# Layer 1 as one stream of 32 attention items, with its layer norms inside

## The chip, the cores and the metric

One core of one Trainium2 chip. The metric is the device time of one execution in microseconds, the median over runs. The kernel before: 1745.28 us, median of 3 runs (1742.61 to 1745.62).

## The reference, cut to what matters

The program is four cross-attention layers in a row on a token tensor of 32 x 64 tokens by 256 (2048 tokens in all), with a context tensor of the same shape. The change is in layer 1:

```
h = layer_norm(x, ln1);  x = x + cross_attention(h, context, w1)     # 16 heads of 128
h = layer_norm(x, ln2);  x = x + cross_attention(h, context, w2)     # same shapes
h = layer_norm(x, ln_mlp); x = x + gelu(h @ w_fc1 + b_fc1) @ w_fc2 + b_fc2   # 256 -> 1024 -> 256
cross_attention: q = h@wq+bq, k = c@wk+bk, v = c@wv+bv, a 65th key and value (bias_k, bias_v) per head
                 softmax(q k / sqrt(128)) v, then @ wo + bo, over groups of 64 queries and 64 keys (+1)
```

Layers 0, 2 and 3 compute other forms of cross-attention; layer 3 ends with an MLP of the same shape as layer 1's. Their arithmetic stays as it is.

## The kernel before, in words

A phase is a set of five instruction streams (one for each engine) between two barriers over all engines. Phases follow one another: setup (`phase_setup`), layer 0 (`phase_layer0`), then for layer 1: features 1, attention 1, features 2, attention 2, features 3 and MLP 1; then the plain features, attention and MLP of layers 2 and 3, and the store.

**Features** (`phase_features`, lines 411 to 629). Four blocks of 512 tokens. DVE aggregates the statistics and normalizes (L590, L597), GpSimd makes the inverse deviation (L502, L504), TensorE transposes 8 squares per block (L524), ScalarE applies scale and offset and rounds to the high part (L559, L565), DVE subtracts to the low part (L607). The attention's features phase also loads its weights and makes 17 bias rows, with 17 float32 products on TensorE (L539, L541; the rows are called `bvo`).

**Attention** (`phase_layer1_attention`, lines 653 to 1016). An item is one block of 512 tokens and one group of 4 heads; 16 items, written out by hand as a pipeline. In iteration j TensorE runs: scores of item j-1 (L772), the first half of context of item j-2 (L828), half the values of item j-1 (L811), the second half of context, the other half of values, outputs of item j-2 (L844), queries and keys of item j (L797). Each float32 product in projections is three products of high and low parts. The context product takes, for each pair of batches and head, two matmuls of 64 rows by 64 columns each (one per batch). DVE turns the probabilities with 16 transposes of 32 partitions per item (L960). In the last group of heads (4 items) TensorE also transposes the kept bias probabilities (L781) and adds one product with `bvo` to each output (L847), and DVE takes the new statistics (L986). GpSimd splits the next group's weights (L722, L724) and SyncE loads them. Every engine takes its work in the order written.

**MLP** (`phase_mlp`, lines 1042 to 1151). TensorE first transposes the bias rows (L1077); then per block 8 products up (L1089), and 8 down (L1101) two steps later. GpSimd adds the second bias to all of `x_res` at the start, and joins the halves of the context.

**Setup** (`phase_setup`). SyncE issues 10 DMAs for the rows of constants (L158), TensorE transposes them (L194), DVE copies them to `cols` (L240), and only then normalizes the tokens for layer 0 (L249).

Of the kernel before, what the change touches and what calls it, by code (L numbers as in the profile page):

```python
# [105 lines left out]
CONST_ROWS = ("bq", "bk", "bias_k", "bias_v", "bv")  # L106


def phase_setup(nc, A, G):
# [4 lines left out]
    with Mem(nc, "su", G.psum) as m:  # L114
# [7 lines left out]
        rows = m.sb("rows", [5 * H1, 2, P])  # L122
# [3 lines left out]
        cols_ps = m.ps("cols_ps", (P, 2, 5 * H1))  # L126
# [8 lines left out]
        rows_in, cols_psum = m.sem("rows_in"), m.sem("cols_psum")  # L135
# [3 lines left out]
        with nc.Block() as block:  # L139
            @block.sync  # L140
            def _(sp):
# [35 lines left out]
            def _(pe):  # L177
# [13 lines left out]

                pe.wait_ge(rows_in, 16 * 2 * len(CONST_ROWS))
                for i in range(2):
                    mm = pe.transpose(cols_ps[:, i, :], rows[:, i, :], G.ident[0:5 * H1, 0:5 * H1])  # L194
# [17 lines left out]
            def _(dve):  # L212
# [27 lines left out]
                dve.tensor_copy(G.cols[:, :, :], cols_ps[:, :, :])  # L240
# [13 lines left out]
def phase_layer0(nc, A, G):  # L254
# [6 lines left out]
    with Mem(nc, "l0", G.psum) as m:  # L261
# [16 lines left out]
        y_psum, y_done, o_psum, x_done = (m.sem(n) for n in ("y_psum", "y_done", "o_psum", "x_done"))  # L278
        STEPS = PAIRS // 2
        with nc.Block() as block:  # L280
            @block.gpsimd
            def _(pool):
                def body(j, front, back):
# [127 lines left out]
def phase_features(nc, G, tag, src, dst_hi, dst_lo, kind, eps=0.0, scale=None, offset=None,  # L411
                   update=False, mlp=None, loads=(), have_stats=True,
                   attention=None):
# [10 lines left out]


    with Mem(nc, tag, G.psum) as m:
        affine = m.sb("affine", [P, 2, KT])
        row_in = m.sb("row_in", [2 * KT, P])
        stats = G.stats if have_stats else m.sb("stats", [P, PAIRS, 6])
        mv = m.sb("mv", [P, PAIRS, 2])  # L430
        rstd = m.sb("rstd", [P, PAIRS])
        normed = m.sb("normed", [P, PAIRS, D])
        raw = [m.sb(f"raw{i}", [P, BLK]) for i in range(2)]
        feat_ps = [m.ps(f"feat_ps{i}", (P, BLK)) for i in range(3)]
        affine_ps = m.ps("affine_ps", (P, 2 * KT))
        affine_in, stats_done, mv_done, eps_added, rstd_done, normed_done = (m.sem(n) for n in
            ("affine_in", "stats_done", "mv_done", "eps_added", "rstd_done", "normed_done"))
        feat_psum, raw_done, hi_done, lo_done = (m.sem(n) for n in ("feat_psum", "raw_done", "hi_done", "lo_done"))
        affine_psum, affine_done, rows_zero = m.sem("affine_psum"), m.sem("affine_done"), m.sem("rows_zero")
        if update:  # L440
            spread_affine = m.sb("spread_affine", [P, 2, D])
            spread_in, scaled = m.sem("spread_in"), m.sem("scaled")
        arrived = m.sem("arrived")
        if attention:
            i_att, wo_dram, bo_dram = attention
            wo, bo = m.sb("wo", [P, H1, D]), m.sb("bo", [1, D])
            lhs, unit = m.sb("lhs", [P, H1, H1 + 1]), m.sb("unit", [1, H1 + 1])
            bvo_ps = m.ps("bvo_ps", (H1 + 1, D))
            wo_in, cleared, unit_zero, lhs_done, bvo_psum = (m.sem(n) for n in
                ("wo_in", "cleared", "unit_zero", "lhs_done", "bvo_psum"))  # L450
        if mlp:
            w_in, w_high = [m.sem(f"w_in{n}") for n in range(2)], m.sem("w_high")
            small_in = m.sem("small_in")
        normalized = src if kind == "plain" else normed
        with nc.Block() as block:
            @block.sync
            def _(sp):
                if scale is not None:
                    sp.wait_ge(rows_zero, 1)
                    sp.dma_start(row_in[0:KT, :], scale.rearrange("(k p) -> k p", p=P)).then_inc(affine_in, 16)  # L460
                    if offset is not None:
                        sp.dma_start(row_in[KT:2 * KT, :], offset.rearrange("(k p) -> k p", p=P)).then_inc(affine_in, 16)
                if update:
                    for n, v in enumerate((scale, offset)):
                        sp.dma_start(spread_affine[:, n, :], v.rearrange("(o n) -> o n", o=1).partition_broadcast(P)).then_inc(spread_in, 16)
                if attention:
                    sp.dma_start(wo[:, :, :], wo_dram.rearrange("(h d) n -> d h n", d=K1)).then_inc(wo_in, 16)
                    sp.dma_start(bo[:, :], bo_dram.rearrange("(o n) -> o n", o=1)).then_inc(wo_in, 16)
# [161 lines left out]

class Operands:
    pass


# [1442 lines left out]
```

## Time and profile before

| | |
|---|---|
| Median of 3 runs | 1745.28 us |
| The profiled execution: time, span | 1738.92 us, 1737.2 us |
| TensorE, busy | 1585.5 us (91%) |
| DVE, ScalarE, GpSimd busy | 1128.0, 668.4, 433.6 us |
| Mean granted TensorE clock | 0.960 |
| First product of attention 1 to first product of MLP 1 | 143.61 to 1153.20 us |

Times within the execution are microseconds from its first instruction. A matmul in float32 is two records of TensorE. "Busy" of TensorE is the union of its records, each of which lasts longer than its share since they overlap: what one costs is read from start to start.

### The profile page before, as it was taken

The page shows a single profiled execution, that of the slowest core. Times are in us where ns is not written, and L with a number is a line of the kernel's source. Part 1 is how long each engine was busy: PE and PEld are TensorE (multiplying, and loading weights), DVE is VectorE, ACT ScalarE, POOL GpSimd, SP SyncE. Part 2 cuts the span into 40 slices and gives each one's busy share as a digit, 9 for nine tenths or more (in the row PEclk, how much of TensorE's full clock was granted, in tenths as well). Part 3 has the DMA queues.
Part 4 walks back from the last instruction along what each step waited for, and adds up shares of the span by engine and source line. Part 5 has one row for each costly group of instructions (what it writes and reads, how often), then busy time and mean ns, then how long its engine had stood idle before and what let it go on. Part 6 is the DMA issues. An engine that isn't in the chain of part 4 may idle for free. (4 is left out here: it accounts for less than half of the span.)

```text
span 1737.2 us, 35121 instructions
## 1 busy us (share of the span) xinstructions
PE 1585.5 (91%) x14252; PEld 1335.9 (77%) x14252; DVE 1128.0 (65%) x2358; ACT 668.4 (38%) x1201; POOL 433.6 (25%) x518
## 2 busy tenths in 40 slices
PE   5979999999999979999999999869878968999797
PEld 3656888888888758888888888758866747888597
DVE  6875666666666655666666666675489955676443
ACT  4654333333333234333333333242256633444321
POOL 2012020110200021110200200081068866763400
PEclk9999999999999979999999999969989978999899
DMA  3011010000000021010000100020140000000001
GB/s 102 1 54 55 2 49 2 25 26 1 25 13 1 1 80 31 19 32 1 26 26 1 38 1 1 1 71 1 17 118 2 2 1 2 2 3 2 1 0 48
DMA packets 48471, 38.35 MB, mean 22 GB/s; under 512 B 10626, under 2 KB 45384, under 8 KB 48200
## 3 DMA queue, kind: packets, MB, share of 16 engines
q1 hardware_dynamic: 48328, 36.30, 7.2%
q8 instruction: 107, 1.75, 0.4%
q14 instruction: 36, 0.29, 0.1%
HBM read 34.20 MB, written 2.10 MB: 21 GB/s over the span
## 5 line engine op out<-in xcount | busy, mean ns | idle before, releaser
L960 DVE STREAM_TRANSPOSE att_pt<-att_prob 32x256 f32<-32x256 f32 x512 | 222.8, 435 | 6.6
L914 ACT ACTIVATE att_q_sb<-psum,split_cols 128x512 f32<-128x512 f32 x128 | 88.1, 688 | 307.7 <-PE psum L797 307.7
L844 PE MATMUL psum<-att_wo_hi,att_ot_hi 128*128 128x256 f32 x512 | 150.4, 294 | 2.8 <-DVE g_x_res L983 2.8
L931 DVE TENSOR_REDUCE att_rmax<-psum 128x6 f32<-128x390 f32 (+1 forms) x96 | 49.2, 513 | 158.1 <-PE psum L772 158.1
L844 PE MATMUL psum<-att_wo_lo,att_ot_hi 128*128 128x256 f32 x512 | 145.8, 285 | 0.0
L844 PE MATMUL psum<-att_wo_hi,att_ot_lo 128*128 128x256 f32 x512 | 145.7, 285 | 0.0
L828 PEld LDWEIGHTS psum<-att_pt,att_v_sb 64*128 64x128 f32 x2048 | 122.2, 191 | 19.3 <-issue 17.7
L828 PE MATMUL psum<-att_pt,att_v_sb 64*128 64x64 f32 x2048 | 131.1, 279 | 4.9 <-DVE att_ot_lo L973 4.9
L917 ACT ACTIVATE att_k_sb<-psum,split_cols 128x512 f32<-128x512 f32 x128 | 88.1, 688 | 92.4 <-PE psum L797 92.4
L973 DVE TENSOR_TENSOR att_ot_lo<-psum,att_ot_hi 128x1024 fp32r<-128x1024 f32 x64 | 78.4, 1225 | 68.2 <-ACT att_ot_hi L880 68.2
L983 DVE TENSOR_TENSOR g_x_res<-psum,g_x_res 128x256 f32<-128x256 f32 x128 | 54.2, 423 | 101.5 <-PE psum L844 78.8
L722 POOL CAST att_wqk_hi<-w_stage_qk 128x512 fp32r<-128x512 f32 x28 | 17.1, 611 | 383.9 <-PE psum L797 382.2
L797 PE MATMUL psum<-split_feat_hi,att_wqk_hi 128*128 128x512 f32 x256 | 102.2, 399 | 6.4 <-POOL att_wqk_lo L741 6.4
L811 PE MATMUL psum<-att_wv_hi,split_ctx_hi 128*128 128x512 f32 x256 | 107.5, 420 | 0.1
L880 ACT ACTIVATE att_ot_hi<-psum 128x1024 fp32r<-128x1024 f32 x64 | 65.6, 1025 | 106.5 <-PE psum L828 106.5
L797 PE MATMUL psum<-split_ctx_hi,att_wqk_hi 128*128 128x512 f32 x256 | 102.2, 399 | 0.0
L844 PEld LDWEIGHTS psum<-att_wo_hi,att_ot_hi 128*128 128x128 f32 x512 | 97.6, 191 | 5.6 <-issue 3.5
L797 PE MATMUL psum<-split_ctx_lo,att_wqk_hi 128*128 128x512 f32 x256 | 101.9, 398 | 0.0
L797 PE MATMUL psum<-split_feat_hi,att_wqk_lo 128*128 128x512 f32 x256 | 101.3, 396 | 0.0
L797 PE MATMUL psum<-split_ctx_hi,att_wqk_lo 128*128 128x512 f32 x256 | 101.3, 396 | 0.0
L797 PE MATMUL psum<-split_feat_lo,att_wqk_hi 128*128 128x512 f32 x256 | 101.1, 395 | 0.0
L811 PE MATMUL psum<-att_wv_hi,split_ctx_lo 128*128 128x512 f32 x256 | 100.9, 394 | 0.0
(292 smaller groups left out, 4059.3 us busy)
## 6 DMA issues: line engine op xcount, KB each, us to landing
ln_wo<-in_L_xattn_wo SPq DMA_DIRECT2D x2, 2048.0 KB
w_stage_qk<-in_L_xattn_wq SPq DMA_DIRECT2D x32, 128.0 KB, 2.3
w_stage_qk<-in_L_xattn_wk SPq DMA_DIRECT2D x32, 128.0 KB, 2.4
w_stage_vo<-in_L_xattn_wv SPq DMA_DIRECT2D x8, 512.0 KB, 4.2
w_stage_vo<-in_L_xattn_wo SPq DMA_DIRECT2D x8, 512.0 KB, 3.9
c_ctx_tok<-in_ctx SPq DMA_DIRECT2D x4, 512.0 KB, 5.2
g_x_res<-in_x SPq DMA_DIRECT2D x4, 512.0 KB, 8.2
m_w<-in_L_xattn_w_fc SPq DMA_DIRECT2D x2, 1024.0 KB, 8.5
```

The source lines that it names most:

```text
L722: pool.tensor_copy(hi, raw).then_inc(w_hi, 1)
L797: mm = pe.matmul(dst[:, :], a, b, start=(k == 0 and t == 0), stop=(k == KT - 1 and t == 2))
L811: mm = pe.matmul(v_ps[p % 2][:, :], a, b, start=(k == 0 and t == 0), stop=(k == KT - 1 and t == 2))
L828: mm = pe.matmul(c_ps[:, u, p % 2, h, :], v_sb[rows, p, h * K1:(h + 1) * K1], pt[rows, h, pp, p % 2, :], start=True, stop=True)
L844: mm = pe.matmul(o_ps[p % 2], a, b, start=(h == 0 and t == 0), stop=(not last and h == HG - 1 and t == 2))
L880: act.activation(by_half(ot_hi, pp), c_ps[:, :, :, :, :].rearrange("p u c h t -> p u (c h) t"), ACT.Copy).then_inc(ot_high, 1)
L914: act.activation(q_sb[:, h, :], q_ps[:, :], ACT.Identity, bias=G.cols[:, i - 1, head:head + 1]).then_inc(q_ready, 1)
L917: act.activation(k_sb[:, h, :, 0:T], k_ps[:, :].rearrange("p (b t) -> p b t", t=T), ACT.Identity, bias=G.cols[:, i - 1, H1 + head:H1 + hea ...
L931: dve.tensor_reduce(rmax[:, a:b], s_ps[group][:, :, :], X_AXIS, ALU.max).then_inc(max_done, 1)
L960: turned = dve.transpose(pt[to:to + 32, :, :, r, 32 * a:32 * a + 32].rearrange("p h a t -> p (h a) t"), by_pair[of:of + 32, :, u, 32 * c:3 ...
L973: dve.tensor_tensor(by_half(ot_lo, pp), c_ps[:, :, :, :, :].rearrange("p u c h t -> p u (c h) t"), by_half(ot_hi, pp).bitcast(F32), ALU.su ...
L983: dve.tensor_tensor(G.x_res[:, pair, :], o_ps[p % 2], G.x_res[:, pair, :], ALU.add).then_inc(x_added, 1)
```

## The change

Layer 1 is one phase, `phase_layer1`, over 32 items (16 per attention), followed by MLP 1. The item pipeline is the one above with these edits.

- The features of a block are made inside the iterations: `norm_at(j)` gives block 0 to 3 at j = -1 to 2, 4 to 7 at j = 15 to 18, 8 to 11 at j = 31 to 34. TensorE transposes the 8 squares after the queries and keys of head 1; ScalarE does 4 operations of 128x512 there; DVE normalizes before it adds outputs; the low part is GpSimd's, in blocks 0 and 11 DVE's. The transposes write into the banks of the scores.
- Bias rows: in the second iteration of each group of heads TensorE makes 4 x 2 rows (`bias_outputs`, 8 float32 matmuls of 2 weight columns each, at partitions 32h), ScalarE copies them, 4 small DMAs place them. The bias probabilities have 33 columns for 17.
- The context product is one matmul of 128 rows by 128 columns per pair of batches and head, with zeros in the blocks off the diagonal; its high and low parts are taken in four steps of 128x512 for two of 128x1024. The outputs wait for all four.
- The last item's probabilities are turned by TensorE and ScalarE.
- The first attention weights are loaded during layer 0; MLP 1's first matrix at the end of the stream, split on ScalarE and GpSimd; its second matrix is split at the start of MLP 1.
- The scales, offsets and MLP biases come as more rows in setup: 8 more DMAs and two more small DVE operations there. The MLPs' own transposes of the bias go.
- In the MLPs GpSimd's additions are spread over the products.

```diff
-            for i in (1, 2):
-                with Mem(nc, f"w{i}") as mw:
-                    w = attention_operands(mw, A, i)
-                    phase_features(nc, G, f"ln{i}", G.x_res, *feat, "ln", 1e-5,
-                                   A[f"L1_xattn_ln{i}_scale"], A[f"L1_xattn_ln{i}_offset"], loads=w.loads,
-                                   attention=(i, A[f"L1_xattn_wo{i}"], A[f"L1_xattn_bo{i}"]))
-                    phase_layer1_attention(nc, A, G, i, w)
-            with Mem(nc, "m1") as mm:
...
-                phase_features(nc, G, "ln3", G.x_res, *feat, "ln", 1e-5,
-                               A["L1_xattn_ln_mlp_scale"], A["L1_xattn_ln_mlp_offset"], mlp=mlp)
-                phase_mlp(nc, G, "mlp1", *feat, mlp, ACT.Gelu, join_context=True, loads=layer2.loads)
+            mlp = layer1_mlp_operands(ms, G, A)
+            phase_layer1(nc, A, G, layer1, mlp)
+            phase_mlp(nc, G, "mlp1", *feat, mlp, G.cols[:, 0, 5 * H1 + 3 * KT:ROWS], ACT.Gelu, join_context=True, split_w2=True,
+                      loads=layer2.loads)
...
+        def norm_at(j):
+            n, b = divmod(j + 1, NG * NBLK)
+            return NBLK * n + b if j >= -1 and b < NBLK and n <= LAYERS else None
...
                 def context(j, pp):
...
                     for p in (2 * pp, 2 * pp + 1):
+                        if pp:
+                            pe.wait_ge(ot_ready, PPB * j + p - 1)
                         for h in range(HG):
-                            for u in range(2):
-                                rows = slice(T * u, T * u + T)
-                                mm = pe.matmul(c_ps[:, u, p % 2, h, :], v_sb[rows, p, h * K1:(h + 1) * K1],
-                                               pt[rows, h, pp, p % 2, :], start=True, stop=True)
-                    mm.then_inc(c_psum, 1)
+                            mm = pe.matmul(c_ps[:, p % 2, h, :], v_sb[:, p, h * K1:(h + 1) * K1],
+                                           pt[:, h, pp, p % 2, :, :].rearrange("p u t -> p (u t)"), start=True, stop=True)
+                        mm.then_inc(c_psum, 1)
...
+                def features(blk, j):
+                    pe.wait_ge(normed_done, PPB * (blk + 1))
+                    if j > 0:
+                        pe.wait_ge(shifted, len(GROUPS) * min(j, NI))
+                    if blk:
+                        pe.wait_ge(raw_done, KT * blk)
+                    if j >= NI:
+                        pe.wait_ge(pt_copied, 4)
+                    for k in range(KT):
+                        for i in range(PPB):
+                            mm = pe.transpose(f_ps[k][:, i * P:(i + 1) * P], normed[:, i, k * P:(k + 1) * P], G.ident[:, :])
+                        mm.then_inc(feat_psum, 1)
+
+                def bias_outputs(g, j):
+                    layer, gl = divmod(g, NG)
+                    pe.wait_ge(wo_ready, g + 1)
+                    pe.wait_ge(shifted, len(GROUPS) * j)
+                    for n, part in enumerate((wo_hi, wo_lo)):
+                        for h in range(HG):
+                            mm = pe.matmul(bvo_ps[32 * h:32 * h + 2, :], G.lhs[:, layer, HG * gl + h, :],
+                                           part[:, h, :].bitcast(F32), start=(n == 0), stop=(n == 1))
+                    mm.then_inc(bvo_psum, 1)
...
+                for j in range(-1, NI + 3):
+                    new, old, now = 1 <= j <= NI, 2 <= j <= NI + 1, norm_at(j)
+                    if new:
                         scores(j - 1)
+                    if old and last_group(j - 2):
+                        turn_bias(j - 2)
+                    if old:
                         context(j - 2, 0)
+                    if new:
                         values(j - 1, 0)
+                    if old:
                         context(j - 2, 1)
+                    if new:
                         values(j - 1, 1)
+                    if j == NI:
+                        turn(NI - 1)
+                    if old:
                         outputs(j - 2)
                     for h in range(HG):
+                        if 0 <= j < NI:
                             queries_keys(j, h)
+                        if h == 1 and now is not None:
+                            features(now, j)
+                        if h == 2 and 0 <= j < NI and j % NBLK == 1:
+                            bias_outputs(j // NBLK, j)
```

ScalarE's operations on a block of features, which stand between its copies of head 1 and of head 2; DVE's order (it stands after the values are kept); and the rows in setup:

```diff
+                def features(blk):
+                    cols = slice(blk % NBLK * BLK, (blk % NBLK + 1) * BLK)
+                    for k in range(KT):
+                        act.wait_ge(feat_psum, KT * blk + k + 1)
+                        if blk:
+                            act.wait_ge(feat_ready, KT * (blk - 1) + k + 1)
+                        scale, offset = affine(blk, k)
+                        act.activation(raw[:, k, :], f_ps[k][:, :], ACT.Identity, bias=offset, scale=scale).then_inc(raw_done, 1)
+                    for k in range(KT):
+                        act.wait_ge(raw_done, KT * blk + k + 1)
+                        act.activation(G.feat_hi[:, k, cols], raw[:, k, :], ACT.Copy).then_inc(hi_done, 1)
...
+                    if now is not None:
+                        normalize_features(now)
                     for p in range(PPB if old else 0):
                         add_output(j - 2, p)
+                    if ahead is not None:
+                        aggregate(ahead)
+                    if now is not None and lows_on_dve(now):
+                        low_features(now)
...
+                    more = [f"L1_xattn_ln{i + 1}_scale", f"L1_xattn_ln{i + 1}_offset", f"L1_xattn_ln_mlp_{('scale', 'offset')[i]}",
+                            ("L1_xattn_b_fc1", "L3_xattn_mlp_b1")[i]]
+                    for n, name in enumerate(more):
+                        at, count = 5 * H1 + KT * n, A[name].shape[0] // P
+                        sp.dma_start(rows[at:at + count, i, :], A[name].rearrange("(k p) -> k p", p=P)).then_inc(rows_in, 16)
```

## Rows read from the trace of the kernel before

**Rows 1.** The page: span, busy time of each engine.
```profile
span 1737.2 us, 35121 instructions
PE 1585.5 (91%) x14252; PEld 1335.9 (77%) x14252; DVE 1128.0 (65%) x2358; ACT 668.4 (38%) x1201; POOL 433.6 (25%) x518
```

**Rows 2.** Windows: stretch, its length, then each engine's busy time, granted clock.
```profile
121.00:143.61 22.61, 13.41 (x67) 7.97 (x68) 15.12 (x46) 12.03 (x19) 8.34 (x16) 0.85 0.45 141
143.61:154.98 11.37, 11.37 (x48) 8.91 (x48) 0.97 (x2) 4.82 (x7) 9.33 (x7) 1.00 0.49 138
154.98:580.89 425.91, 425.87 (x3633) 366.38 (x3632) 280.65 (x602) 150.77 (x227) 44.34 (x39) 1.00 0.05 15
580.89:622.70 41.81, 35.84 (x337) 32.18 (x336) 25.13 (x52) 8.53 (x14) 0.00 (x0) 0.88 0.00 1
622.70:648.13 25.43, 15.33 (x68) 8.53 (x68) 15.98 (x48) 12.03 (x19) 8.34 (x16) 0.78 0.40 125
1087.95:1127.80 39.85, 33.84 (x337) 30.22 (x336) 25.12 (x52) 8.52 (x14) 0.00 (x0) 0.96 0.00 1
1127.80:1153.20 25.40, 8.08 (x34) 6.73 (x34) 19.75 (x43) 15.07 (x22) 15.49 (x13) 0.58 0.26 89
317.81:346.53 28.72, 28.72 (x249) 24.82 (x248) 18.61 (x40) 10.12 (x15) 5.71 (x6) 1.00 0.11 29
549.90:580.89 30.99, 30.99 (x261) 26.62 (x260) 20.31 (x44) 10.66 (x17) 0.00 (x0) 1.00 0.00 1
```

**Rows 3.** Timeline of TensorE: start, duration, instruction (scores of two items).
```profile
580.89 2.09 PE L772 MATMUL psum<-att_k_sb,att_q_sb 128*64 128x65 f32 x64
681.23 0.45 PE L772 MATMUL psum<-att_k_sb,att_q_sb 128*64 128x65 f32 x8
```

**Rows 4.** Timeline of TensorE: context, outputs, products of 128 and 32 weight columns.
```profile
319.82 2.00 PE L828 MATMUL psum<-att_pt,att_v_sb 64*128 64x64 f32 x32
329.53 0.28 PE L844 MATMUL psum<-att_wo_hi,att_ot_hi 128*128 128x256 f32 x1
1472.30 0.61 PE L1390 MATMUL psum<-narrow_feat_f,l_wk 128*128 128x128 f32 x4
1472.75 0.61 PE L1390 MATMUL psum<-g_ctx_f,l_wk 128*128 128x128 f32 x4
1293.59 1.08 PE L1844 MATMUL psum<-l_pt,l_v_bd 128*32 128x128 f32 x32
133.82 2.33 PE L539 MATMUL psum<-ln_wo,ln_lhs 128*17 128x256 f32 x10
132.80 1.09 PE L524 MATMUL psum<-g_ident,ln_normed 128*128 128x128 f32 x8
```

**Rows 5.** Groups by line: busy, mean ns of one, idle before.
```profile
L559 ACT ACTIVATE ln_raw<-psum,ln_affine 128x512 f32<-128x512 f32 x24 | 18.4, 768 | 16.7 <-PE psum L524 14.5 <-DVE split_feat_lo L607 2.2
L565 ACT ACTIVATE split_feat_hi<-ln_raw 128x512 fp32r<-128x512 f32 x24 | 15.1, 631 | 0.8
L914 ACT ACTIVATE att_q_sb<-psum,split_cols 128x512 f32<-128x512 f32 x128 | 88.1, 688 | 307.7 <-PE psum L797 307.7
L504 POOL TENSOR_TENSOR ln_rstd<-ln_rstd,g_minus_half 128x4 f32<-128x4 f32 x12 | 13.5, 1127 | 1.0
```

**Rows 6.** Timeline of DVE: alone, beside GpSimd, and in an item.
```profile
1135.43 0.69 DVE L607 TENSOR_TENSOR split_feat_lo<-ln_raw,split_feat_hi 128x512 fp32r<-128x512 f32 x1 [1.29 <-ACT split_feat_hi L565]
1140.71 5.60 DVE L607 TENSOR_TENSOR split_feat_lo<-ln_raw,split_feat_hi 128x512 fp32r<-128x512 f32 x2
1146.24 1.37 DVE L597 TENSOR_SCALAR ln_normed<-g_x_res,ln_mv,ln_rstd 128x256 f32<-128x256 f32 x4
327.82 1.23 DVE L973 TENSOR_TENSOR att_ot_lo<-psum,att_ot_hi 128x1024 fp32r<-128x1024 f32 x1 [0.51 <-ACT att_ot_hi L880]
```

**Rows 7.** Timeline of setup: the last DMA of rows, and who waits.
```profile
22.79 0.42 SPq L158 DMA_DIRECT2D su_rows<-in_L_xattn_bv  x1
25.19 0.33 DVE L240 COPY split_cols<-psum 128x160 f32<-128x160 f32 x1 [0.96 <-PE psum L194]
```

More of the change, by code:

```diff
@@ L527, in _ @@
-                if scale is not None:
-                    pe.wait_ge(affine_in, 16 if offset is None else 32)
-                    pe.transpose(affine_ps[:, :], row_in[:, :], G.ident[0:2 * KT, 0:2 * KT]).then_inc(affine_psum, 1)
-                for b in range(NBLK):
-                    feature_block(b)
-                    if attention and b:
-                        if b == 1:
-                            pe.wait_ge(lhs_done, 2)
-                            pe.wait_ge(cleared, 3)
-                            pe.wait_ge(wo_in, 32)
-                        for h in range(H1 * (b - 1) // (NBLK - 1), H1 * b // (NBLK - 1)):
-                            pe.matmul(bvo_ps[:, :], lhs[:, h, :], wo[:, h, :], start=(h == 0), stop=False)
@@ L540, in _ @@
-                if attention:
-                    pe.matmul(bvo_ps[:, :], unit[:, :], bo[:, :], start=False, stop=True).then_inc(bvo_psum, 1)
+                for n in range(NBLK * KT):
+                    b, k = divmod(n, KT)
+                    if n >= 3:
+                        pe.wait_ge(moved, n - 2)
+                    for i in range(PPB):
+                        mm = pe.transpose(feat_ps[n % 3][:, i * P:(i + 1) * P], src[:, PPB * b + i, k * P:(k + 1) * P], G.ident[:, :])
+                    mm.then_inc(feat_psum, 1)
@@ L701, in _ @@
             def _(sp):
-                for g in range(NG):
+                for g in range(NGROUP):
+                    layer, gl = divmod(g, NG)
                     for h in range(2 if g == 0 else 0, HG):
@@ L775, in scores, with turn @@
                             mm.then_inc(s_psum, 1)
+                def turn(j):
+                    pe.wait_ge(shifted, len(GROUPS) * (j + 1))
+                    pe.wait_ge(prob_ready, len(GROUPS) * (j + 1))
+                    for pair in range(2):
+                        for h in range(2):
+                            for pp in range(2):
+                                n = PPB * (2 * pair + h) + 2 * pp
+                                mm = pe.transpose(t_ps[pair][:, h, pp, :], prob[:, n:n + 2, :].rearrange("p c t -> p (c t)"), G.ident[:, :])
+                        mm.then_inc(t_psum, 1)
                 def turn_bias(j):
@@ L888, in _ @@
                 act.wait_ge(bp_zero, 1)
-                for j in range(NI + 2):
-                    new, old = 1 <= j <= NI, j >= 2
+                for j in range(-1, NI + 3):
+                    new, old, now = 1 <= j <= NI, 2 <= j <= NI + 1, norm_at(j)
                     if new:
@@ new lines, in _ @@
+                    for h in range(HG):
+                        if 0 <= j < NI:
+                            projected(j, h)
+                        if h == 1 and now is not None:
+                            features(now)
+                        if h == 2 and 0 <= j < NI and j % NBLK == 1:
+                            act.wait_ge(bvo_psum, j // NBLK + 1)
+                            if j > 1:
+                                act.wait_ge(bvo_in, 64 * (j // NBLK))
+                            act.activation(bvo_raw[:, :], bvo_ps, ACT.Copy).then_inc(bvo_kept, 1)
@@ L1094, in down @@
                     pe.wait_ge(act_ready, FT * j + f + 1)
+                    if split_w2 and first and f % (FT // 2) == 0:
+                        pe.wait_ge(w2_ready[f // (FT // 2)], 1)
                     for p in range(PPB):
```

680 lines of the change are left out of this document (325 added, 355 removed).

## The prediction

> **What bounds the kernel now.** I read the page first: TensorE is busy 1585.5 of 1737.2 us [rows 1], so only its idle or slow time, or fewer products, can give much. The windows then say where that time lies. Between the second item's scores and the last one's, each attention is full: 425.87 of 425.91 us busy, clock 1.00; an inner item takes 28.72 us and an item of the last head group 30.99 us, both without a gap, while DVE is busy 18.61 and ScalarE 10.12 us of the 28.72 [rows 2]. The rest of layer 1 is loose. The first features phase takes 22.61 us. After the last scores of an attention 41.81 and 39.85 us pass, and the features phases behind them take 25.43 and 25.40 us with TensorE busy 15.33 and 8.08, much of it at the lower clock (0.78 and 0.58 of full, i.e. a mix of 2.4 and 1.2 GHz) [rows 2]. The change removes three such joints. What it can win is there; what it can lose is in the 32 items, where every nanosecond put on TensorE's list is on the path.
>
> **The join of the two attentions.** From the scores of item 15 (580.89) to the scores of the second attention's second item (681.23) 100.34 us pass [rows 3]. In one stream these are two ordinary iterations with last-group outputs, 2 x 30.99 = 61.98 us [rows 2]. That saves 38.4 us before anything is added.
>
> **What enters the items.** Features of a block: 8 transposes; eight took 1.02 us from start to start at full clock (132.80 to 133.82), and 0.87 if they follow with no other work in between; I take 0.9 [rows 4]. Behind them ScalarE has two scalings (0.768 each) and two roundings (0.631) in the middle of the copies of queries and keys (0.688 each) [rows 5]. Count from the first transpose: the key copy of head 1 ends at 0.8, the four operations at 3.6, the query copy of head 2 at 4.3. TensorE after its transposes and the two 1.4 us products of head 2 (48 records, eight products, in 11.37 us, [rows 2]) wants that bank at 3.7: a stall of 0.6 us. Later copies are in time again. So 1.5 us per block, for seven blocks inside full iterations (2 to 8) 10.5; DVE's normalizing (1.37 for four, [rows 6]) before the output additions adds perhaps 0.5 once: 11 us. The bounds are 6 (no stall) and 18 (each step 1.7 instead of 0.9 and a full ScalarE block of 2.8 hidden by half only).
>
> Bias rows: 8 groups, each 8 float32 matmuls of 256 moving columns, 16 records. The nearest row with four column positions of 32 took 1.08 us for 32 records of 128 columns, that is four at a time; doubled columns and half the records give 1.1 us by the same rate, I take 1.0 [rows 4]. Sum 8. If they don't run side by side, the row with 17 weight columns says 2.33 us for 10 records, 3.7 for 16 [rows 4]: 30 in all. The wait before them, for the split of the output weights, is covered: the split starts when outputs end, and three heads of queries and keys (three quarters of the 11.37 us, 8.5) lie between. ScalarE's copy and the small DMAs come 4 us before anyone needs them.
>
> Context: 32 records of 64x64 took 2.00 us to the end of the last, 62 ns per record [rows 4]. Now 16 records of 128 columns replace them. The nearest row, full height and 128 columns, has four in 0.45 us (1472.30 to 1472.75), 112 ns each [rows 4]: 1.79 us for the half, and 0.16 more until the last one ends (four lasted 0.61 where they took 0.45 of the list), 1.95. No gain and no loss, 0 per item; bounds -0.1 and +0.4 us. The Trainium skill speaks against the edit here ("TensorEngine Tiling (Array Packing)", Theoretical Speedup): half-height work packed into two row tiles may run up to twice as fast as unpacked, so giving packing up would double these 4.0 us per item. The case's records don't show that packing paid: two half-height records take 125 ns together, no less than the 112 of one full-height record.
>
> Waits moved in the item: outputs of an item now wait for all four low parts. The second DVE low part ended at 329.05 and TensorE started outputs at 329.53 [rows 4, 6], so even the old grain would just do; in four steps of about 0.69, each starting as soon as its 128x512 is copied, the last one ends earlier. Nothing. DVE has 10 us of slack per item and ScalarE 18 [rows 2], which covers two more instructions each. GpSimd was busy 5.71 us of that item and none of the last-group one [rows 2], so the features' low parts and the splits have most of an item before their use.
>
> **The start.** In setup DVE already waits 0.96 us for the copied rows [rows 7], and the last row DMA is the last thing SyncE issues. Eight more at 0.3 to 0.42 us each [rows 7] push it, and with it layer 0, by 3.0; two more DVE operations with a wait by 0.5: +3.5 us (bounds 2.5 and 4.5). Then the first features: the old phase takes 22.61 us [rows 2] and the scores of item 0 start at 154.98, 34.0 after the barrier. New: GpSimd's inverse deviation (1.127, [rows 5]) ends at 2.7, behind two small operations; normalizing takes 1.4 to 3.4 (GpSimd is splitting weights beside it, and DVE beside GpSimd took 2.8 for what takes 0.69 alone [rows 6]), the transposes 1.7 at the lower clock, scaling and rounding, low parts: first product at 12 us. The features of block 1 then wait until DVE has split the value weights and cleared the larger `pt` (about 20 us after the barrier), and head 3 follows at 24, so that the scores of item 0 start at 27.5: -6.5 us (bounds -11 and -2).
>
> **The end.** Old: 65.25 us from the last scores (1087.95) to MLP 1 (1153.20) [rows 2]. New: last-group iteration without queries 21.5 (turning by TensorE 0.9 included), transposes of block 9 at 22.2, context of item 31. Its copies stand on ScalarE behind the features of block 9 (2.8) and the two halves of the first MLP matrix (an estimate of 2.1, from 0.631 for 128x512), so outputs start at 31.8, as late as before (31.0). They end at 39.5. Then serially: last addition and statistics 0.9, inverse deviation 1.5, normalizing 2 to 3.4 beside GpSimd's low part, transposes 1.7, ScalarE 2.8, low part 0.7, barrier 0.3: MLP at 51. -14 us (bounds -16 and -8). The second matrix's split lies beside the first three products up: 0. Each MLP loses its bias transposes, for MLP 3 -0.5.
>
> **Sum**, against the profiled execution of 1738.92 us: -38.4 + 11 + 8 + 0 + 3.5 - 6.5 - 14 - 0.5 = -36.9, to 1702. That execution was 6.4 below the median of 1745.28; the same difference taken from the median gives 1708.4, and I say 1708.
>
> **The rivals.**
>
> A. The bias rows run one after another: 22 us more than I count, 1730. For it: the only row with fewer than 32 weight columns (17) shows 233 ns per record, though all wrote to one place. Against: the four positions of L1844 did overlap [rows 4].
>
> B. The layer norms don't fit: if each of the 12 blocks makes TensorE wait for the whole of ScalarE's four operations (2.8) instead of 0.6, or DVE and GpSimd hold each other in every block as they did in the third features phase [rows 6], 12 to 15 us more, 1721. For it: the order on each engine is fixed, with the four operations in the middle of copies that TensorE waits for. Against: the count above, with ScalarE's slack.
>
> C. The joints give all they can: no ScalarE stall, a start and an end at their lower bounds, 1697.
>
> D. Slower: the full-height context product costs more than the packed pair. The place is L828, the price 32 items x 32 records x what a record takes beyond 112 ns; the gain of 37 us is gone at 36 ns, a record of 148. That would be so if a weight load of 128 columns no longer hid behind 128 moving columns: at 224 ns, double, it is 115 us and 1823. Against: full-height records at 112 ns in [rows 4]. The packing rule of the Trainium skill ("TensorEngine Tiling (Array Packing)", Theoretical Speedup) would give the same doubling.
>
> E. The change doesn't do what it says: TensorE still waits at the joint between item 15 and 16, because feature blocks 4 to 7 need the outputs of items 12 to 15. The outputs of item 12 come one iteration before its block's transposes and two before its queries, so only a full iteration's delay (31 us) would show; it would give 1739.
>
> **Chances.** My forecast 0.66, A 0.10, B 0.12, C 0.06, D 0.04, E 0.02. For 8 in 10 the range is 1697 to 1728: my case with the bounds of its terms, C, B and most of A. A measurement of this kernel can tell about 0.2% (3.5 us) from no change. Forecast, A, B and C are all faster; D is slower, E about even: 0.93 faster, 0.02 same, 0.05 slower.
>
> **What would show each step.** The scores of neighbouring items 31.0 to 33 us apart right across item 16, clock 1.00 throughout; context halves of 2.0 us with 16 records; 16 bias records in about 1 us (3.5 if A holds); a gap of about 0.6 us before the query product of head 3 in iterations with features; the first scores about 3 us earlier than 154.98, the MLP about 51 us after the last scores. Wrong: a context half over 2.4 us, a gap at item 16, DVE as releaser of outputs, or layer 0 shifted by more than 5 us.

## The result

The changed kernel takes 1674.26 us, median of four runs (1673.19 to 1674.98), against 1745.45 us for the kernel before (1742.61 to 1745.77): ratio 0.9599, 95% interval 0.9584 to 0.9614. I had said 1708, 1697 to 1728. The direction was right, the size was not: 71 us came where I counted 37, and the time lies outside my range.

The page of the changed kernel, answering to [rows 1]:

```profile
span 1672.4 us, 33255 instructions
PE 1545.5 (92%) x13291; PEld 1321.8 (79%) x13291; DVE 1103.6 (66%) x2377; ACT 672.5 (40%) x1270; POOL 454.6 (27%) x533
```

The windows of the changed kernel, answering to [rows 2]: an inner item, one of the last head group, one of these with a features block, from the scores of item 15 to those of item 17, and from the last scores to the MLP.

```profile
285.06:313.05 27.99, 27.99 (x217) 24.71 (x216) 18.84 (x42) 10.25 (x17) 0.00 (x0) 1.00 0.07 20
511.41:541.46 30.05, 30.05 (x229) 26.56 (x229) 20.99 (x50) 10.89 (x19) 1.27 (x2) 1.00 0.07 19
541.46:572.89 31.43, 31.23 (x238) 27.32 (x237) 22.20 (x54) 13.13 (x23) 5.27 (x6) 1.00 0.00 1
572.89:637.87 64.98, 63.68 (x490) 54.87 (x489) 46.72 (x108) 26.66 (x47) 20.78 (x20) 1.00 0.09 26
1040.27:1090.71 50.44, 37.25 (x305) 34.40 (x305) 27.74 (x64) 20.58 (x37) 12.12 (x10) 0.90 0.08 25
```

The reader is to see two things. The joint is gone: 64.98 us instead of 100.34 [rows 3], clock 1.00, TensorE busy all but 1.3 us, of which one wait of 1.11 at 589.49. And the inner item, which I had left at 28.72 us, takes 27.99 though nothing idle was in it before; the last-group item fell from 30.99 to 30.05. The timeline of TensorE, answering to [rows 3, 4]: the last stage of layer 0, the first scores, the two context halves of an item, a group's bias rows, and at the end the first outputs of item 31 and the first product of MLP 1.

```profile
122.33 0.44 PE L349 MATMUL psum<-l_prob_t,l_y 128*64 128x256 f32 x2 [0.83 <-ACT l_prob_t L374]
149.47 0.28 PE L694 MATMUL psum<-att_k_sb,split_q_sb 128*64 128x65 f32 x2
287.08 2.05 PE L764 MATMUL psum<-att_pt,att_v_sb 128*128 128x128 f32 x16
291.75 1.95 PE L764 MATMUL psum<-att_pt,att_v_sb 128*128 128x128 f32 x16
281.14 0.61 PE L807 MATMUL psum<-att_wo_hi,split_lhs 128*2 128x256 f32 x8
281.57 0.61 PE L807 MATMUL psum<-att_wo_lo,split_lhs 128*2 128x256 f32 x8
1071.90 0.39 PE L781 MATMUL psum<-att_wo_hi,att_ot_hi 128*128 128x256 f32 x1 [1.41 <-DVE att_ot_lo L977]
1090.71 0.77 PE L1139 MATMUL psum<-split_feat_hi,split_wide_hi 128*128 128x512 f32 x1 [2.98 <-PEq L564]
```

Where the 64.8 us between the two spans lie, against the terms of my sum:

| stretch | forecast | measured | off by |
|---|---|---|---|
| first scores to last scores (31 intervals) | -38.4 + 11 + 8 = -19.4 | 932.97 to 890.80: -42.2 | -22.8 |
| up to the first scores | +3.5 - 6.5 = -3.0 | 154.98 to 149.47: -5.5 | -2.5 |
| last scores to MLP 1 | -14 | 65.25 to 50.44: -14.8 | -0.8 |
| MLP 1 | 0 | 95.7 to 93.2: -2.5 | -2.5 |
| the rest | -0.5 | +0.2 | +0.7 |

The remaining 6 us of my miss are the offset of 6.4 that I carried from the profiled execution to the median; the changed kernel's profiled execution (1674.09 us) is at its median. The old kernel's executions differ with the granted clock: 1735.54 us at 0.962 and 1750.23 at 0.953 in one series, 1738.92 at 0.960 here. The part up to the first scores is also larger than this one trace says: in four variants of the old kernel (e3, e4, e10, e12) the first scores came at 157.3 to 159.4, at a granted clock of 0.74 to 0.83 between 115 and 155 us, where this trace has 0.91.

So one number needs a cause: 22.8 us over 31 items, 0.74 us each. Item by item, from start to start: context halves 3.51 us instead of 3.86, values 5.73 instead of 5.85, outputs 5.75 and 5.76, queries and keys 10.99 instead of 11.25. The last of these in windows, of the kernel before (queries and keys, the first values):

```profile
306.56:317.81 11.25, 11.25 (x51) 8.85 (x49) 7.31 (x17) 4.82 (x7) 0.00 (x0) 1.00 0.00 0
293.03:295.99 2.96, 2.96 (x14) 2.17 (x12) 1.80 (x4) 1.93 (x3) 0.00 (x0) 1.00 0.00 0
```

and of the changed kernel:

```profile
302.06:313.05 10.99, 10.99 (x50) 8.82 (x48) 7.30 (x17) 4.83 (x7) 0.00 (x0) 1.00 0.00 0
288.88:291.75 2.87, 2.87 (x16) 2.35 (x15) 2.52 (x6) 1.82 (x4) 0.00 (x0) 1.00 0.18 52
```

The products of queries and keys are the same in both kernels, 48 records of 512 columns; only their tiles lie elsewhere. After the first six records of each item's queries and keys it is 226 to 227 ns from record to record now. It was 228 to 240, and not the same for both: 231 on average in the products with features (queries), 235 in those with context (keys).

### The profile page after: what moved, and what is told of

Same layout as the page of the kernel before. It is cut to its first block and busy times, and to the rows that moved or that the text cites. A ratio compares the mean times of both kernels' runs of the same rounds, so it can differ in the third digit from the quotient of the medians.

```text
span 1672.4 us, 33255 instructions
## 1 busy us (share of the span) xinstructions
PE 1545.5 (92%) x13291; PEld 1321.8 (79%) x13291; DVE 1103.6 (66%) x2377; ACT 672.5 (40%) x1270; POOL 454.6 (27%) x533
## 5 line engine op out<-in xcount | busy, mean ns | idle before, releaser
L764 PE MATMUL psum<-att_pt,att_v_sb 128*128 128x128 f32 x1024 | 128.6, 279 | 3.5 <-DVE att_ot_lo L977 3.5
L764 PEld LDWEIGHTS psum<-att_pt,att_v_sb 128*128 128x128 f32 x1024 | 122.9, 193 | 7.9 <-DVE att_ot_lo L977 3.7
L732 PE MATMUL psum<-split_feat_hi,split_wide_hi 128*128 128x512 f32 x256 | 103.7, 405 | 4.5 <-DVE split_feat_lo L1011 3.3
L746 PE MATMUL psum<-att_wv_lo,split_ctx_hi 128*128 128x512 f32 x256 | 100.6, 393 | 0.0
L732 PE MATMUL psum<-split_feat_lo,split_wide_hi 128*128 128x512 f32 x256 | 100.5, 393 | 0.0
L732 PE MATMUL psum<-split_feat_hi,split_wide_lo 128*128 128x512 f32 x256 | 100.3, 392 | 0.0
L732 PE MATMUL psum<-split_ctx_hi,split_wide_hi 128*128 128x512 f32 x256 | 99.9, 390 | 0.0
L732 PE MATMUL psum<-split_ctx_lo,split_wide_hi 128*128 128x512 f32 x256 | 99.8, 390 | 0.0
L732 PE MATMUL psum<-split_ctx_hi,split_wide_lo 128*128 128x512 f32 x256 | 99.6, 389 | 0.0
L781 PEld LDWEIGHTS psum<-att_wo_lo,att_ot_hi 128*128 128x128 f32 x512 | 97.9, 191 | 2.0
```

The costliest lines, as they stand in the source:

```text
L732: mm = pe.matmul(dst[:, :], a, b_, start=(k == 0 and t == 0), stop=(k == KT - 1 and t == 2))
L746: mm = pe.matmul(v_ps[p % 2][:, :], a, b, start=(k == 0 and t == 0), stop=(k == KT - 1 and t == 2))
L764: mm = pe.matmul(c_ps[:, p % 2, h, :], v_sb[:, p, h * K1:(h + 1) * K1], pt[:, h, pp, p % 2, :, :].rearrange("p u t -> p (u t)"), start=Tru ...
L781: mm = pe.matmul(o_ps[p % 2], a, b, start=(h == 0 and t == 0), stop=(not last and h == HG - 1 and t == 2))
```

## The experiments

Two theories, F (the full-height context is cheaper) and P (the place of a tile in memory sets the pace of products that nobody changed), each undone in the new kernel and done alone in the old one. For F this was done with the whole context part, that is the products and the grain of their copies together (e1, e4); e11 tells the two apart.

**e1_pairs.** The context as in the kernel before, all else changed.

```
-  mm = pe.matmul(c_ps[:, p % 2, h, :], v_sb[:, p, ...], pt[:, h, pp, p % 2, :, :] as (u t), ...)
+  for u in range(2):
+      mm = pe.matmul(c_ps[:, u, p % 2, h, :], v_sb[rows, p, ...], pt[rows, h, pp, p % 2, u, :], ...)
+  (context_high, context_low: one 128x1024 step per half)
```

> The changed kernel with one part undone: the context product is again two 64-row products side by side per head and pair (32 records a half), into two banks, copied in one 128x1024 step per half. Theory F (full height is cheaper): the halves go from 1.8 and 1.7 us back to 1.93 each, 0.35 us per item, 32 x 0.35 = 11 us, so 1685 us; queries and keys stay at 227 ns a record. Rival G (the item got shorter for another reason and the halves only shrank because of what runs beside them): halves stay under 1.8 us, time within 1672 to 1677. Rival H (the finer copies, four of 128x512, are what helps): halves at 1.8 but a gap before the second half or before outputs.

Measured: 1698.51 us, ratio 0.9739 (0.9706 to 0.9771), 24 over the changed kernel. Its windows: an inner item, item 15 to 17, the end.

```profile
287.91:316.41 28.50, 28.50 (x250) 24.80 (x249) 18.62 (x40) 10.13 (x15) 0.00 (x0) 1.00 0.07 20
581.13:650.24 69.11, 66.86 (x553) 56.36 (x553) 47.33 (x104) 26.22 (x43) 21.03 (x20) 0.98 0.08 24
1060.30:1115.83 55.53, 39.72 (x369) 36.02 (x369) 27.20 (x60) 20.14 (x33) 12.12 (x10) 0.85 0.07 22
```

The item is 0.51 longer (I had 0.35: I had left out the values behind each half), and the two loose stretches are 4.1 and 5.1 us longer, which I hadn't expected.

**e4_before_full.** The other way round: the kernel before with this part alone.

> The kernel before with the context part of the change alone: one product of full height per head and pair against a zero-filled block, four copies of 128x512. Theory F: 0.35 us per item less, 1734. Rival G: no change, 1745. My first forecast had 0 with bounds of -0.1 and +0.4 us an item, that is 1742 to 1758.

Measured: 1721.19 us, 0.9874 (0.9836 to 0.9912), so -22. The item:

```profile
289.39:317.62 28.23, 28.23 (x219) 24.73 (x218) 18.84 (x42) 10.24 (x17) 0.00 (x0) 1.00 0.01 1
```

28.73 less 0.50, the same step as in e1, and rival G falls. A last-group item loses 0.70 (30.29 us), and from the scores of item 15 to those of item 16 it takes 76.65 us instead of 81.15, which theory F alone doesn't give. That the inner item's 0.50 belongs to the products and not to the finer copies is shown by e11.

**e2_after_off64, e3_before_off64.** One line each, `ms.sb("pad", [P, 16])`, ahead of `q_sb` in the changed kernel and ahead of the features in the kernel before.

> The changed kernel with 64 bytes of padding before q_sb, so that all tiles of the attention behind it (weights of queries and keys among them) start at an odd multiple of 64 bytes instead of a multiple of 128. Theory P (place in memory sets the record's time): queries and keys go from 227 to about 231 to 234 ns a record, 48 records x 4 to 7 ns x 32 items = 6 to 11 us, so 1680 to 1685. Rival Q (the pitch depends on what else runs, not on the place): 227 ns and 1674.

> The kernel before with 64 bytes of padding before the feature tiles, so that features, weights and all attention tiles start at a multiple of 128 bytes. Theory P: queries and keys fall from 230 to 236 ns a record to 227, 0.35 us per item, 11 us in all: 1734. Rival Q: 1745 and the old pitch.

Measured: 1683.34 us (0.9656, 0.9623 to 0.9688), 9 over the changed kernel, item 28.34, records 233 to 234 ns. Moving tiles by 64 bytes costs 0.35 us an item. But the pad in the old kernel gave nothing: 1745.15 (1.0008, 0.9991 to 1.0024). So the place matters, and "a multiple of 128" is the wrong rule. The next two measured the rule by itself.

**e5_places, e6_grid.**

> Not the computation of the reference: 1000 float32r products on zero-filled tiles, 18 in a row for each pair of places (weights 0, 64, 128, 256, 384 bytes past a multiple of 512; moving operand 0, 64, 256), with 512 and with 256 moving columns, first with the other engines idle, then with DVE and ScalarE at 128x512 operations all the time. Theory P2 (weights that start at a multiple of 512 bytes are read faster): 227 ns from record to record at offset 0 and 231 to 236 at the others, whatever the moving operand's place. Theory P3 (the moving operand decides): the pitch follows the moving offset. Rival Q (the place doesn't matter, other engines' accesses do): one pitch in the idle half, a longer one in the busy half.

> Not the computation of the reference: float32r products on zero-filled tiles in the kernel's own order (high-high, high-low, low-high, four weight tiles), 12 in a row for each of 64 pairs of places (weights and moving operand each 0 to 448 bytes past a multiple of 512, in steps of 64), with 512 and then with 256 moving columns, nothing else running. Theory P2: with 512 columns 226 to 227 ns where the weights start at a multiple of 256, 229 to 236 elsewhere; with 256 columns the other way round, 120 ns where both start at a multiple of 256 and about 114 where the moving operand stands 192 bytes past the weights. Rival: in this order the places average out and all pairs lie within 2 ns.

e5: the 270 products of 512 columns took 62.33 us with the other engines idle and 62.47 with DVE and ScalarE busy throughout, and each pair of places had the same pace in both halves but for one record: it is not contention with these two engines (GpSimd and DMA were not run). P2 and P3 both fail as rules: with the moving operand at 0, weights at 256 had the same 226.6 as weights at 0, weights at 64, 128 and 384 about 233; and with weights at 0 the moving operand's places 64 and 256 had 230. e5 and e6 are one execution each. Windows of e5, idle and busy:

```profile
29.17:91.50 62.33, 62.33 (x271) 50.70 (x270) 0.00 (x0) 0.00 (x0) 0.00 (x0) 1.00 0.00 1
124.36:186.83 62.47, 62.47 (x270) 50.80 (x271) 59.55 (x86) 59.48 (x95) 0.00 (x0) 1.00 0.00 1
```

e6, five of its 128 groups of 12: 512 columns with weights and moving operand at (0, 0), (64, 0), (192, 128); 256 columns at (64, 64), (64, 256).

```profile
23.15:25.87 2.72, 2.72 (x13) 2.25 (x12) 0.00 (x0) 0.00 (x0) 1.00 0.03 6
45.32:48.12 2.80, 2.80 (x14) 2.25 (x13) 0.00 (x0) 0.00 (x0) 1.00 0.00 0
95.23:98.04 2.81, 2.81 (x13) 2.26 (x12) 0.00 (x0) 0.00 (x0) 1.00 0.00 0
213.40:214.84 1.44, 1.44 (x15) 1.44 (x13) 0.00 (x0) 0.00 (x0) 1.00 0.00 0
217.67:219.03 1.36, 1.36 (x15) 1.36 (x13) 0.00 (x0) 0.00 (x0) 1.00 0.00 0
```

Four rows of the grid, ns from record to record (first start to twelfth, over 11), by the moving operand's place:

```
512 columns        0     64    128    192    256    320    384    448
weights at   0 226.6  230.4  233.1  232.9  228.5  230.4  233.0  232.8
weights at  64 233.3  228.5  230.4  233.0  232.9  228.5  230.4  233.1
256 columns
weights at   0 118.9  118.1  118.5  115.5  118.2  118.2  118.5  115.6
weights at  64 117.5  120.2  117.9  117.7  113.4  118.3  118.1  118.5
```

Mostly the distance counts: with 512 columns the pace is best where moving operand and weights stand a multiple of 256 bytes apart, and 226.6 only with both at 0. With 256 columns most pairs have 118; 113.3 to 113.4 comes at four of the 64 pairs, weights and moving operand at (64, 256), (192, 128), (320, 256) and (448, 128), while others at the same distances have 115.5 to 117.5. The order of the products counts as well: the pair (256, 0) has 230.5 here and had 226.6 in e5. P2 was right on the size and half right on the rule. The grid explains the two pads by the tiles' offsets modulo 512, added up from the order of allocation: in the changed kernel weights are at 0, context at 256, features at 0 (228.5 and 226.6 in the grid, 227 in the kernel); in e2 weights at 64 (233 in the grid, 233 in the kernel); in the kernel before weights at 320, context at 0, features at 192 (233 in the grid for both, 235 and 231 in the kernel); in e3 384, 0 and 256 (232 to 233, no gain). So it fits to about 2 ns.

**e10_before_places.** The kernel before, padded by that rule (`[P, 80]` ahead of the features, `[P, 96]` ahead of `wqk_hi`).

> The kernel before with padding so that features, context and the weights of queries and keys all start at a multiple of 512 bytes (the pad of 64 bytes tried first had put them at 256, 0 and 384, where the grid shows no gain). Theory P2: queries and keys fall from 230 to 236 ns a record to 227, the item from 28.73 to 28.45 us, 9 us in all, 1736. Rival: 1745.

Measured: 1737.55 us, 0.9964 (0.9948 to 0.9979), the expected sign and two thirds of the size; records 226 to 227 ns after the first nine, item:

```profile
292.33:320.84 28.51, 28.51 (x250) 24.80 (x249) 18.60 (x40) 10.13 (x15) 0.00 (x0) 1.00 0.01 1
```

**e12_before_two.** Both in the kernel before.

> The kernel before with the two small parts together: full-height context with the finer copies, and features, context and weights of queries and keys at multiples of 512 bytes. If they add up (22.5 and 6 us alone, items 28.73 - 0.50 - 0.24 = 27.99 us), 1716 us, and what is left to the changed kernel's 1674 is what my steps without the context counted: 42 against my 37. Rival (they share a cause, a late start of TensorE's queue after the context): 1721.

Measured: 1714.07 us, 0.9832 (0.9808 to 0.9855). They add up, and the item is the changed kernel's to the hundredth:

```profile
290.16:318.15 27.99, 27.99 (x218) 24.73 (x217) 18.82 (x42) 10.24 (x17) 0.00 (x0) 1.00 0.00 1
```

**e11_coarse.** Full height kept, copies and waits per half as before; it splits what e1 had undone in one.

> The changed kernel with the full-height context products kept, but copied and waited for as in the kernel before, in one 128x1024 step per half. It tells apart the two halves of what the context part gave. Theory F+H: the full height gives the inner items (0.50 us each, halves 1.8 and 1.7 us, values behind them 0.12 shorter) and the finer copies give the loose stretches (4.1 us where the attentions join, 4.4 at the end): inner items stay at 28.0, the time is 8 us over the changed kernel, 1682. Rival F alone: 1674 to 1676, and the loose stretches as in the changed kernel. Rival H alone: items back at 28.5, 1698.

Measured: 1694.28 us, 0.9718 (0.9693 to 0.9744), 20 over the changed kernel, outside all three. Most inner items are at 28.00, as F says, and with that the 0.50 us is the products' alone. But five (3, 7, 11, 19, 27), in each of which GpSimd begins to split the value weights 11.55 us behind the scores, take 30.1 or 31.6; item 23, whose split begins at 11.85, takes 28.00. Windows of item 3 and of item 5:

```profile
229.07:260.66 31.59, 29.75 (x217) 26.12 (x216) 21.39 (x40) 10.12 (x15) 5.54 (x5) 0.95 0.11 34
289.87:317.87 28.00, 28.00 (x218) 24.59 (x217) 18.61 (x40) 10.12 (x15) 0.00 (x0) 1.00 0.08 20
```

DVE in item 3 of e11, then GpSimd there:

```profile
240.72 1.21 DVE L949 TENSOR_TENSOR att_prob<-att_soft,att_rinv 128x256 f32<-128x256 f32 x1
241.86 2.36 DVE L969 TENSOR_TENSOR att_bias_prob<-att_soft,att_rinv 128x16 f32<-128x16 f32 x1
244.13 0.68 DVE L980 COPY att_v_sb<-psum 128x512 f32<-128x512 f32 x1
247.56 0.42 DVE L985 TENSOR_TENSOR g_x_res<-psum,g_x_res 128x256 f32<-128x256 f32 x1 [2.09 <-PE psum L781]
...
240.62 1.04 POOL L600 CAST att_wv_hi<-g_ctx_f 128x1024 fp32r<-128x1024 f32 x1 [8.89 <-PE psum L746]
241.75 2.43 POOL L603 TENSOR_TENSOR att_wv_lo<-g_ctx_f,att_wv_hi 128x1024 fp32r<-128x1024 f32 x1
```

TensorE in the same item, at its outputs, and the window behind that wait:

```profile
245.20 0.39 PE L781 MATMUL psum<-att_wo_hi,att_ot_hi 128*128 128x256 f32 x1 [1.84 <-DVE g_x_res L985]
245.89:249.24 3.35, 3.35 (x18) 3.35 (x17) 0.42 (x1) 0.00 (x0) 0.00 (x0) 0.51 0.38 130
```

The same in the changed kernel:

```profile
238.51 0.43 DVE L951 TENSOR_TENSOR att_prob<-att_soft,att_rinv 128x256 f32<-128x256 f32 x1
238.85 0.18 DVE L971 TENSOR_TENSOR att_bias_prob<-att_soft,att_rinv 128x16 f32<-128x16 f32 x1
...
239.43 1.04 POOL L600 CAST att_wv_hi<-g_ctx_f 128x1024 fp32r<-128x1024 f32 x1 [8.86 <-PE psum L746]
```

With the finer copies DVE is through with its two multiplications at 239.03, 0.4 us before GpSimd starts. With the coarse ones the first starts 0.1 us after GpSimd: 0.43 becomes 1.21, 0.18 becomes 2.36, and the value copy and the output additions are late. The item is 3.6 us longer. For 2.1 of it TensorE's outputs wait for their bank. Behind this wait the granted clock is 0.51, and 16 records of outputs take 213 ns from start to start instead of 120, which costs the other 1.5. Items 7 and 27 have the wait alone (30.09).

The Trainium skill has the rule ("SBUF — State Buffer", Who interferes with whom): a DVE instruction with two inputs in SBUF and a GpSimd instruction that reads SBUF contend for a port that one of them holds for its whole instruction, and the later one waits. The rows agree for a DVE instruction that comes second: the multiplication of 128x16 ends at 244.22, GpSimd's at 244.18. In e1 GpSimd comes second, 0.07 us behind the multiplication of 128x256, and its split takes 1.25 us instead of 1.04.

It matters which of the two starts first. The multiplication of 128x256 starts 0.91 us ahead of GpSimd's split in the changed kernel, 0.20 ahead in the kernel before, 0.07 in e1 and 0.19 in e11's item 23. In the last three the second multiplication takes 1.02 instead of 0.18, which costs the item nothing. In the five long items it starts 0.11 behind.

So the finer copies are worth about 20 us in this kernel, and not for the reason that I gave them (a start a little earlier). By the trace, of an execution that was the slowest of e11's five (1699.15 us), it is 17 us in the stream, 15.0 of them in the five items, and 6 at the end (56.60 us instead of 50.44, at a granted clock of 0.83 instead of 0.90). Full height with coarse copies is 4 us under e1, and the two intervals overlap: the products give their 0.50 us an item, and the collisions that this brings take it back.

**e8_tail, e7_layout, e9_both.** Could more be had? e8 changes the order at the end, e7 the places by the grid, e9 both.

> The changed kernel with another order at its end: the transposes of layer-norm block 10 ahead of the last outputs, the split of the first MLP matrix behind the last context copies on ScalarE (and behind that block on GpSimd). My account of the end (outputs of item 31 wait because ScalarE does two scalings, two roundings and two 128x1024 copies before the context copies): outputs start at 28.5 instead of 31.64 after the last scores, the MLP at 45.5 instead of 50.44, 1669 us. Rival (the end hangs on DVE and GpSimd, which hold each other up when both run): outputs earlier but the MLP still after 49.5, 1673.

Measured: 1672.54 us, 0.9578 (0.9553 to 0.9602), 1.7 us under the changed kernel, less than the spread of its own five runs (1668.24 to 1675.05). In the trace the MLP comes 48.1 us after the last scores, where the changed kernel has 50.4 and I expected 45.5. DVE's normalizing, put first, ran beside GpSimd (3.27 us for four instead of 1.37) and held up the low parts, so that outputs started at 31.0 instead of 28.5:

```profile
1063.92 3.27 DVE L1007 TENSOR_SCALAR g_ctx_f<-g_x_res,att_mv,att_rstd 128x256 f32<-128x256 f32 x4 [1.47 <-POOL att_rstd L637]
1067.12 1.27 DVE L980 TENSOR_TENSOR att_ot_lo<-psum,att_ot_hi 128x512 fp32r<-128x512 f32 x2
```

> The changed kernel with nothing but padding and the order of its memory tiles changed, by the grid measured before: features, context and the weights of queries and keys at a multiple of 512 bytes, value weights too, output weights at 256 and the context outputs (stationary side) at 64 bytes past one, and in both MLPs the first matrices at 0, second matrix at 256, activations at 64. Theory P2: outputs go from 120 to 113.5 ns a record (48 records, -0.31 us an item), values from 231 to 227 (24 records, -0.1), 32 x 0.41 = 13 us; in each MLP 384 records down at 113.5 instead of 119 and 192 up at 227 instead of 232, 3 us; in all 19 us, 1655. Rival Q2 (inside the kernel the other engines' accesses set the pitch): under 4 us, 1670 or more.

Measured: 1669.13 us, 0.957 (0.955 to 0.9589), 5 under the changed kernel where 19 were expected. Values came to 226 to 227 ns after the first six to eight records of a half, but outputs only from 120 to 118, not to 113.5: the item is 27.83. The grid doesn't carry over to products of 256 columns; why is open. The end gained nothing: outputs 31.8 and MLP 52.1 us after the last scores.

> The same layout and the other order at the end in one kernel, with DVE's normalizing of block 10 behind its first two low parts instead of ahead of them (ahead, it held them up until 26.1 us after the last scores, and two of its four operations took 1.35 us beside GpSimd). If both hold and don't share time: the layout's gain, and the MLP 46 us after the last scores instead of 50.44, 1651 us.

Measured: 1663.13 us, 0.9528 (0.9507 to 0.9548), 11 us under the changed one. It is 12 over the 1651 expected, since the layout gave 5 and not 19. Outputs of item 31 start 28.1 and the MLP 44.9 us after the last scores (1035.81), which is the order's doing, as the layout alone left both late (e7):

```profile
1063.94 0.39 PE L784 MATMUL psum<-att_wo_hi,att_ot_hi 128*128 128x256 f32 x1 [0.48 <-DVE att_ot_lo L982]
1080.73 0.76 PE L1149 MATMUL psum<-split_feat_hi,split_wide_hi 128*128 128x512 f32 x1 [2.98 <-PEq L566]
```

## Why the prediction was wrong, step by step

**The context, "0 per item": wrong, and this is the step that failed.** I had the pace right: 112 ns a record, 16 in 1.79 us, and the half took 1.80. Then I added 0.16 us "until the last one ends". Nobody waits for that end: the values' first product starts 0.24 us before the last full-height record ends, and only 0.07 before the end of the last packed pair. So the halves are 1.80 and 1.71 against 1.93, and the values behind them 0.12 shorter (why, no run shows): 0.50 us an item, 15.5 in 31 intervals. With its copies in four steps the whole context part is worth more, 22 us in the old kernel (e4) and 24 in the new one (e1); in the old one the rest lies mostly at the joint of the two attentions. My bounds, -0.1 and +0.4, both leaned on that tail and left the gain out. Rival D, with the packing rule of the Trainium skill ("TensorEngine Tiling (Array Packing)", Theoretical Speedup), pointed the other way: here the packed pair costs 121 ns (1.93 us for 16 pairs), one full-height record 112. The rule compares packed half-height work with unpacked half-height work; one full-height product over a zero-filled block is neither, so the doubling that I drew from it doesn't follow.

**What isn't in my sum: the place of the tiles.** I took the 11.25 us of queries and keys as fixed because no product changed. It lost 0.24 us an item, 7.4 in the stream, because the change puts their weights into a shared tile at another address (e10, e12). The trace of the kernel before had a sign of it that I didn't look for: queries and keys are the same product, with the moving operand at two places, and went at 231 and 235 ns a record.

**The joint, -38.4: right.** 64.98 us is two last-group items (60.1), two features blocks, a group's bias rows and 1 us of waits. The wait of 1.11 us is DVE's and GpSimd's: DVE normalizes block 4 beside the split of the value weights, four operations take 3.79 us instead of 1.37, and the output addition behind them is late:

```profile
585.31 3.79 DVE L1004 TENSOR_SCALAR g_ctx_f<-g_x_res,att_mv,att_rstd 128x256 f32<-128x256 f32 x4
585.92 2.38 POOL L603 TENSOR_TENSOR att_wv_lo<-g_ctx_f,att_wv_hi 128x1024 fp32r<-128x1024 f32 x1
```

Rival E is out: TensorE doesn't wait for the features of blocks 4 to 7.

**Features, 1.5 a block: right.** An item with one takes 1.39 more (29.38 to 27.99), 0.79 of it the transposes. But the stall of 0.6 ahead of head 3 is 0.2, and the first products behind the transposes and behind the stall are slower by 0.4 together, which I hadn't counted: that the sum comes out is partly luck. Rival B is out. Its price was also mis-added: 2.2 us more in each of 12 blocks is 26, and the 15 that I gave belongs to the seven blocks inside full iterations.

**Bias rows, 1.0 a group: nearly.** 16 records from 281.14, 0.98 us, so side by side, and the item is 1.20 longer; rival A is out.

**Setup, +3.5: right.** Layer 0's last products start at 122.33 instead of 118.65, +3.7:

```profile
118.65 0.44 PE L332 MATMUL psum<-l_prob_t,l_y 128*64 128x256 f32 x2 [0.83 <-ACT l_prob_t L357]
```

**The start, -6.5: too small.** The scores of item 0 come 27.1 us behind that row instead of 36.3, -9.2, inside my bounds. No run takes it apart.

**The end, -14: right, and for the reasons given.** Outputs at 31.6 (I said 31.8), the MLP at 50.4 (51). e9 confirms ScalarE's and DVE's order as the cause (28.1 and 44.9), e8 only in part. What I didn't see is that this rests on the copies in four steps (e1: 55.5, e11: 56.6).

**Waits, "nothing": wrong on what is at stake.** In the changed kernel's inner items nothing waits, as I said; but "DVE has 10 us of slack" was no argument: at one place DVE starts 0.9 us ahead of GpSimd, the finer copies give 1.0 us there, and 20 us hung on it.

**MLP 1, 0:** 2.5 us shorter; the cause is open. **MLP 3, -0.5:** nothing. **The chances:** those of the faster cases add up to 0.94, not 0.93.

What is left when both item effects are given to the old kernel: e12's 1714.1 to 1674.3, 40 us, for which my other terms had 37. So the sum was short by what the two effects give, 30 us by e12 (1743.67 to 1714.07 in its series), and by 3 or 4 elsewhere.

## What to carry to other kernels

Count a block of products from its first start to the first start of what follows: a tail that the next product overlaps is no cost. Slack is a matter of a place, not of an item: for each pair of DVE and GpSimd operations on SBUF data ask which starts first and by how much, and what a shift of a microsecond would do. And when tiles are re-allocated, products that nobody touched may change pace by 3%; work out the offsets of weights and moving operand modulo 512 bytes. For 512 columns both at 0 was the best place here; for 256 columns these runs give no rule that held in the kernel.

## What was unexpected of the hardware

The pace of a float32r product depends on the places of its two operands modulo 512 bytes: 226.6 to 234.4 ns with 512 columns, 113.3 to 120.2 with 256, the same whether DVE and ScalarE work or not (e5). A DVE multiplication of 128x16 that takes 0.18 us alone took 2.36 behind a GpSimd split.
